# A three-layer graph network: own rows turned by transposing DMAs and joined by VectorE, in place of identity products and ScalarE copies

## What is computed

```
agg0 = segment_mean((x[src] + rel_emb[type]) @ W_msg.T + b_msg, dst)
x1   = layernorm(x + x @ W_self.T + b_self + agg0)                      # layer 0
h    = swish(segment_mean(x1[src], dst) @ W1_l.T + b1 + x1 @ W1_r.T)    # layer 1
out  = layernorm(x1 + segment_mean(h[src], dst) @ W2_l.T + b2 + h @ W2_r.T)   # layer 2
```

## Time and profile before

| | |
|---|---|
| time, median of 3 runs | 354.44 us (354.37 to 354.53) |
| time of the profiled execution | 354.82 us |
| its span in the profile | 353.0 us (1.8 us lie around it) |
| TensorE busy | 327.9 us, 93% |
| VectorE busy | 232.5 us, 66% |
| ScalarE busy | 172.2 us, 49% |
| granted TensorE clock, mean | 0.994 |

### The profile page before, as it was taken

The page is one execution under the profiler, slowest core; times in us unless marked ns, Lnnn a source line. Parts: engine busy times, 40 slices in busy tenths (PEclk is TensorE's granted clock), DMA queues, the critical chain, the costliest instruction groups (busy, mean ns, idle before and its releaser), DMA issues.

```text
span 353.0 us, 9059 instructions
## 1 busy us (share of the span) xinstructions
PE 327.9 (93%) x3319; PEld 244.3 (69%) x3319; DVE 232.5 (66%) x597; ACT 172.2 (49%) x380; POOL 4.9 (1%) x18
## 2 busy tenths in 40 slices
PE   0699999999999999999999999999999999999990
PEld 0698788998998998998994645554564655554560
DVE  6999999989999999999447893213307225225304
ACT  3586557778878778778712422312322411211220
POOL 5000000000000000000000000000000000000000
PEclk9999999999999999999999999999999999999997
DMA  4712000000000000000110000000000001001011
GB/s 138 241 32 62 2 2 9 2 4 9 3 2 8 3 2 9 3 4 2 39 42 8 2 0 0 2 0 2 0 2 1 2 30 31 2 30 31 2 32 37
DMA packets 6958, 7.30 MB, mean 21 GB/s; under 512 B 653, under 2 KB 5888, under 8 KB 6912
## 3 DMA queue, kind: packets, MB, share of 16 engines
q1 hardware_dynamic: 6624, 6.25, 6.0%
q10 hardware_dynamic: 288, 0.43, 0.3%
HBM read 4.75 MB, written 1.60 MB: 18 GB/s over the span
## 4 chain that ended last, share of the span: by engine, by line
PE 82%; DVE 5%; ACT 2%; issue 1%; ACTq 0%; DVEq 0%
PE ps L1021 37%; PE ps L1002 17%; PE ps L947 15%; PE ps L1095 5%; PE ps L1105 3%; PE ps L1040 2%; ACT counts L891 1%; DVE hot L1258 1%; PE ps L954 1%; PE ps L964 1%; DVE table L1268 1%; DVE hot L1251 0%; DVE table L1258 0%; ACT new_first L869 0%; DVE table L1330 0%
## 5 line engine op out<-in xcount | busy, mean ns | idle before, releaser
L1021 PE MATMUL ps<-counts,table 128*128 128x512 f16 (+1 forms) x736 | 135.2, 340 | 0.0
L891 ACT CAST counts<-ps 128x494 f32 x208 | 107.7, 579 | 44.1 <-PE ps L947 43.6
L1021 PEld LDWEIGHTS ps<-counts,table 128*128 128x128 f16 x736 | 60.5, 97 | 64.8 <-issue 0.2
L947 PE MATMUL ps<-hot 128*128 128x156 f16 (+1 forms) x592 | 68.9, 241 | 13.8 <-DVE hot L1258 13.3
L1002 PE MATMUL ps<-counts,table 128*128 128x256 f16 x600 | 78.2, 271 | 0.0
L947 PEld LDWEIGHTS ps<-hot 128*128 128x128 f16 x592 | 53.4, 102 | 16.9 <-DVE hot L1258 14.6
L1258 DVE TENSOR_TENSOR hot<-iota,edges 128x1200 f16<-128x1200 f16 x74 | 57.5, 777 | 0.0
L1002 PEld LDWEIGHTS ps<-counts,table 128*128 128x128 f16 x600 | 52.9, 97 | 5.5
L954 PE MATMUL ps<-window_hot,hot 128*128 128x19 f16 x296 | 43.0, 180 | 0.0
L1251 DVE TENSOR_TENSOR hot<-iota,edge_rows 128x768 f16<-128x768 f16 x74 | 40.8, 551 | 2.8 <-PE ps L984 2.3
L847 ACT ACTIVATE scaled<-ps,rdeg 128x128 f32<-128x128 f32 (+1 forms) x75 | 21.7, 373 | 24.0 <-PE ps L1095 21.6
(11 more groups left out here) (148 smaller groups left out, 324.4 us busy)
## 6 DMA issues: line engine op xcount, KB each, us to landing
own_T<-x_turned SPq DMA_DIRECT2D x4, 256.0 KB, 2.7
table<-x_rows SPq DMA_DIRECT2D x1, 832.0 KB, 5.9
table<-x_rows SPq DMA_DIRECT2D x1, 768.0 KB, 4.2
out<-new_first SPq DMA_DIRECT2D x3, 256.0 KB
out<-hot SPq DMA_DIRECT2D x3, 256.0 KB, 2.4
sum_first<-x_turned SPq DMA_DIRECT2D x2, 256.0 KB, 4.9
counts<-counts SPq DMA_DIRECT2D x6, 53.0 KB
counts<-first_dst ACTq DMA_DIRECT2D x1, 208.0 KB, 3.8
```

The costliest lines, as they stand in the source:

```text
L891: nc.scalar.copy(A[:, HALVES[half], bass.ds(bases[group % 8], GROUP_W)], window(group, half)).then_inc(copied[half], 1)
L947: return nc.tensor.matmul(window(group, half)[:, :, at[t]], row(tiles[t], LOW_AT, P), blocks_of(tiles[t], half), start=group == half == t ...
L1021: last = nc.tensor.matmul(ps[:, sums_bank(q), 0:nodes], table[:, b, which, :], A[:, b, at:at + nodes], start=b == which == 0, stop=b + 1 = ...
```

## The change

The identities (`ident_h`, `ident_stacked`), `turn` on TensorE and `turn_out` on ScalarE go. SP turns the rows instead: `turn_rows(q)` issues, per tile of 128 nodes, one transposing DMA within SBUF for the high part and one for the low part, 8 a chunk (one for the short chunk, where one tile holds both), into `turned_high` and `turned_low`. These lie on what the counting used (`window_hot` and `iota`), so the first ones wait for `opened`, TensorE's last reading of `iota`. There is one such pair of buffers; `turn_rows(q)` waits until the chunk before has been joined (`own_ready`). VectorE joins: `join(q)` adds the two parts in float16 into `x_T(q)` in float32. The division by 256 moves to the weights that meet these rows: one VectorE operation on `weights_later[:, 1:4:2]` at q = 6.

`join(q + 1)` stands in VectorE's iteration q after `add_up(q)`, ahead of `swish` or `measure`; for the short chunk ahead of `preset(q + 1)`.

```
+            def turn_rows(q):
+                sp.wait_ge(lo_ready, q - CHUNKS + 1)
+                if q > CHUNKS:
+                    sp.wait_ge(own_ready, q - CHUNKS)
+                first = chunk_of(q) * SUB
+                for t in range(tiles_of(q)):
+                    sp.dma_start(turned_high[:, t * P:(t + 1) * P],
+                                 table_in(q)[:, first + t, 0, :], transpose=True
+                                 ).then_inc(turned, 16)
+                    if tiles_of(q) > 1:
+                        sp.dma_start(turned_low[:, t * P:(t + 1) * P],
+                                     table_in(q)[:, first + t, 1, :], transpose=True
+                                     ).then_inc(turned, 16)
...
             stack_counts(EARLY + 1)
+            sp.wait_ge(opened, OPENED)
+            for q in range(CHUNKS, 2 * CHUNKS + 2):
+                turn_rows(q)
             for q in range(2 * CHUNKS, ALL_CHUNKS):
+                if q + 2 < ALL_CHUNKS:
+                    turn_rows(q + 2)
                 sp.wait_ge(rows_ready, q + 1)
...
+            def join(q):
+                dve.wait_ge(turned, turned_by(q))
+                if tiles_of(q) > 1:
+                    dve.wait_ge(dense_done, q)
+                    high, low_bits = turned_high, turned_low
+                else:
+                    dve.wait_ge(messages_done, before(q) + 1)
+                    high = turned_high[:, 0:LAST]
+                    low_bits = turned_high[:, REL_ROW:REL_ROW + LAST]
+                nc.vector.tensor_tensor(x_T(q)[:, 0:nodes_of(q)], high, low_bits, ALU.add
+                                        ).then_inc(own_ready, 1)
...
             for q in range(EARLY - 1, ALL_CHUNKS):
                 if EARLY <= q < CHUNKS:
                     degrees(q)
+                if q == CHUNKS - 1:
+                    dve.wait_ge(late_weights_in, 80)
+                    nc.vector.tensor_scalar(weights_later[:, 1:4:2, :], weights_later[:, 1:4:2, :],
+                                            1.0 / SCALE, None, ALU.mult
+                                            ).then_inc(weights_ready, 1)
...
+                joins = CHUNKS <= q + 1 < ALL_CHUNKS
+                if joins and tiles_of(q + 1) == 1:
+                    join(q + 1)
                 if q + 1 < ALL_CHUNKS:
                     preset(q + 1)
                 add_up(q)
+                if joins and tiles_of(q + 1) > 1:
+                    join(q + 1)
```

Removed in return:

```
-            def turn_out(q):
-                act.wait_ge(turned, q + 1 - CHUNKS)
-                nc.scalar.copy(x_T(q)[:, 0:nodes], ps[:, TURN, 0:nodes]
-                               ).then_inc(own_ready, 1)
-            def turn(q):
-                for t in range(tiles_of(q)):
-                    for part in range(1 if both else 2):
-                        last = nc.tensor.matmul(
-                            ps[:, TURN, t * P:t * P + size],
-                            table_in(q)[:, chunk_of(q) * SUB + t, part, :],
-                            ident_stacked if both else ident_h[:, 0:size],
```

More of the change, by code:

```diff
@@ L181, in summed_before @@
     return q - 1 if q <= EARLY else -1 if q == EARLY + 1 else q - 2
+OPENED = 1
 def stored_in(slot):
@@ L221, in gnn_program @@
         bias_first = sb("bias_rows", [P, 2, D])
-        ident_h = sb("ident_h", [P, P], F16)
         rel_ones = sb("rel_ones", [P, 2], F16)
@@ L261, in gnn_program @@
         bias_last = later[:, 4 * D + 2 * CHUNK + TILES + GROUPS:][:, 0:D]
-        ident_stacked = later[:, 5 * D + 2 * CHUNK + TILES + GROUPS:].bitcast(F16)[:, 0:LAST]
-        assert 5 * D + 2 * CHUNK + TILES + GROUPS + P // 4 <= (SLOTS - 1) * HOT_C * GROUP // 2
+        assert 5 * D + 2 * CHUNK + TILES + GROUPS <= (SLOTS - 1) * HOT_C * GROUP // 2
+        turned_high = window_hot[:].rearrange("p n h w t -> p (n h w t)")[:, 0:CHUNK]
+        turned_low = iota[:].rearrange("p c t -> p (c t)")[:, 0:CHUNK]
         ident = new_first[:, 0:P]
@@ L284, in x_T, with turned_by @@
             return own_T[:] if tiles_of(q) > 1 else sum_T(q)[:, P:P + LAST]
+        def turned_by(q):
+            full = q - CHUNKS + 1 - sum(tiles_of(k) == 1 for k in range(CHUNKS, q + 1))
+            return 16 * (2 * SUB * full + q - CHUNKS + 1 - full)
         def new(q):
@@ L317, in sums_bank @@
             return 4 if q <= EARLY or slot_of(q) else 0
-        TURN = 3
         def messages_bank(q):
@@ L843, in scale @@
                 else:
-                    act.wait_ge(weights_ready, 3)
+                    act.wait_ge(weights_ready, 2)
                 for t in range(tiles_of(q)):
@@ L913, in _ @@
                     lead(q)
-                    if q >= CHUNKS:
-                        turn_out(q)
                 if q > EARLY:
@@ L1027, in aggregate @@
                         last.then_inc(agg_done, 1)
-            def turn(q):
[L1030 to L1036, removed]
-                for t in range(tiles_of(q)):
-                    size = min(P, nodes_of(q))
-                    for part in range(1 if both else 2):
-                        last = nc.tensor.matmul(
-                            ps[:, TURN, t * P:t * P + size],
-                            table_in(q)[:, chunk_of(q) * SUB + t, part, :],
-                            ident_stacked if both else ident_h[:, 0:size],
-                            start=part == 0, stop=both or part == 1, skip_group_check=True)
-                last.then_inc(turned, 1)
             def wait_turned(q):
@@ L1089, in dense @@
                     if q == CHUNKS:
-                        pe.wait_ge(late_weights_in, 80)
+                        pe.wait_ge(weights_ready, 3)
                     if q >= POSTED:
@@ L1152, in _ @@
                     aggregate(q, range(cut, BLOCKS))
-                    turn(q)
                 else:
                     aggregate(q, range(BLOCKS))
-                    turn(q)
                     dense(q - 1, all_tiles(q - 1))
@@ L1281, in constant @@
                                             ALU.add).then_inc(weights_ready, 1)
[L1282 to L1286, removed]
+            CONSTANTS = (4, 14)
             def degrees(k):
@@ L1312, in preset @@
                 else:
-                    dve.wait_ge(opened, 1)
+                    dve.wait_ge(opened, OPENED)
                 if layer < 2:
@@ L1530, in _ @@
             wait_copied(dve, GROUPS)
-            nc.vector.tensor_tensor(ident_stacked, ident_h[:, 0:LAST],
-                                    ident_h[:, REL_ROW:REL_ROW + LAST], ALU.add
-                                    ).then_inc(weights_ready, 1)
             nc.vector.memset(table1[32:REL_ROW, BLOCKS - 1], 0.0)
```

3 lines of the change are left out of this document (removed).

## The result

The changed kernel takes 356.33 us (355.82 to 356.99, 5 runs) against 354.53 (5 runs) for the kernel before: a ratio of 1.0047 with an interval of 1.0029 to 1.0065. It is slower by half a per cent, where 350.6 was forecast and a range of 349.9 to 372.

A forecast was written before the change was run, and what follows sets the result against it. TensorE was taken to bound the kernel: 4.46 us of later turns removed, less 0.61 us net delay at dense(8), gave 354.44 - 3.85 = 350.6 us, with cheap DMAs assumed; range 349.9 to 372.

The forecast's parts named there:

- What bounds the kernel: TensorE, busy in nearly every slice and 82% of the last chain, sets the pace at 12.80 us a chunk.
- the work removed: On TensorE, each full chunk's eight turn products give 0.44 us, 5.3 us over 12 chunks; short chunks 0.03 us twice.
- The work added on VectorE: Join 0.69 us and scaling 0.40 delay TensorE 1.09 us at layer 1's start; dense(8) starts 0.61 later, net.
- The spacing c: Spacing of eight transposing DMAs on SP's queue: bounds 0.47 and 2.0 us, taken as below 0.83, near plain DMAs.
- The price at a given c: At join(7), each 0.1 us of c beyond 0.83 costs 0.7 us; beyond 1.37, the cycle costs 8.4 us.
- rival C: Nothing gained, c from 1.28 to just past 1.37: first stall or cycle eats the gain, 353.7 to 355.1; chance 0.09.
- This happens once: The first batch's lateness at join(7) stalls TensorE only once, since everything behind shifts with it.
- The ring's own sum: Join, eight DMAs, join: cycle 7c + 2.77 us from 186.5 to join(19), against TensorE's 12.36; slack used up near c 1.32.
- A: Cheap transposes, c up to 0.83: 350.6 us, or 350.2 to 351.5 with variations; chance 0.45.
- D: Transposes become the bound, c over 1.37, ring longer than TensorE's chunk: 366 us at c 1.5, 408 at 2.0; chance 0.33.
- What the profile after was to show: Layer 1 lead spacing 12.36 us, join 0.69, TensorE idle about 1 us before aggregate(7)'s last block, eight issues from 186.5.

The follow-up runs named there:

- run 2: Changed kernel without transposing DMAs, joins or weight scaling, TensorE multiplying old buffer contents: 349.61 us, ratio 0.9861 to the kernel before.
- run 1: Changed kernel without its 98 transposing DMAs and the join's wait for them, the join adding old contents: 350.87 us, ratio 0.9895 to the kernel before.
- run 13: Changed kernel with one transposing DMA for a whole chunk, 1024 columns to eight blocks: 350.54 us, ratio 0.9889 to the kernel before.
- run 12: Changed kernel with one transposing DMA for a tile's high and low part, 50 DMAs in all: 350.17 us, ratio 0.9876 to the kernel before.
- run 5: Changed kernel with the first eight DMAs issued early and join(7) and join(14) behind low(q): 351.92 us, ratio 0.9925 to the kernel before.
- run 8: Changed kernel with only join(14) moved behind low(13): 356.59 us, ratio 1.0056 to the kernel before.
- run 11: Changed kernel with each full-chunk transposing DMA turning only 64 of its tile's 128 rows: 356.51 us, one run.
- run 6: Changed kernel with first eight DMAs early, join(7) and join(14) behind low(q), and two pairs of buffers: 351.73 us, ratio 0.9911 to the kernel before.

## Why the prediction was wrong

- **What bounds the kernel, and the work removed.** Right. TensorE alone set the pace; the chunks now follow at 12.36 us, and the removal alone gives 1.4% (run 2).
- **The work added on VectorE.** Right in place, too dear in size. The join takes 0.69 us as forecast (0.691 measured) and 0.20 in place of 0.40 of the scaling shows, but `low(6)` is delayed by 0.69 us in all, not 1.09, and TensorE by 0.45 at `dense(7)` and 0.66 at `dense(8)` (runs 1 and 2, each counted from its `dense(5)`). The slack there was not nil: the prediction's own 196.01 against 196.23 leaves 0.2 us. Counted so to `dense(19)` the kernel without DMAs gains 4.4 us where 3.85 was forecast. That its median, 350.87, lies so close to the 350.6 of the sum is in part luck.
- **The spacing c: the step that failed first.** "I take c near the plain spacing, below 0.83". It is 1.27, from a fixed cost of each issue on SP. The argument "32 KB over sixteen engines that are idle" looked at the wrong resource: the engines were indeed idle, and the bytes cost next to nothing (run 13 moves eight times as much in the same 1.24 us), but the issuing queue was busy for 1.23 us. The prediction itself called c a choice and not a reading. The figure of 1309 ns that the prediction quoted from the Trainium skill ("VectorE: DVE Perf Modes", "The three transpose paths") was the better guide, near the 1.27 of the trace; but that is the spacing of issues, while a block has landed 2.4 us after its issue, and eight blocks in one DMA are issued in 1.24. The other page's statement, transposes as fast as regular DMAs ("Advanced Engine Details and Errata", "X-Bar Transpose (TRN2)"), says nothing of issues, and for them the trace has 1.27 against 0.47.
- **The price at a given c: two terms missing.** With c = 1.27 and a landing of 2.4 us the prediction's own formula gives 350.6 + 7 x 0.44 + 0.4 = 354.1, and its rival C reached to 355.1; 356.3 was measured. Missing is first the low clock behind a stall of 4 us: 1.6 us by `dense(7)`, about 1.1 after the give-back. The prediction let the stall cost its own length. Missing is second the deadline in the middle. It asked the ring to be in time for `dense(19)`; but `join(14)` stands ahead of `low(13)`, which TensorE awaits at layer 2's start, 0.9 us. With both the sum is 356.1. "This happens once" was true of the first batch and overlooked the second place of the same form.
- **The ring's own sum.** The prediction adds two short chunks of 2.35 us ahead of `join(19)`, but only q = 13 lies there, so its slack used up at c = 1.32 should read 1.35. With c = 1.27 and a landing of 2.4 the corrected sum has `join(19)` end at about 333.9 us, in time; it started at 339.05. The sum lacks the pause at `join(8)`, which came 3.0 us behind the ring because the edge checks stand ahead of it, and five issues that took 3.8 us more than the others. A cycle without such an issue is mostly 11.96 us (212.60 to 224.56), with one 12.6 to 13.0, against TensorE's 12.36: the ring had next to nothing to catch up with.
- **The rivals.** The result is C's mechanism, a late first join that eats the gain, plus these two terms. A's time is that of the kernel without DMAs and of run 12. D would have needed c over 1.37 by the prediction's arithmetic; at 1.27 its ring was already felt, by 0.9 us in the kernel after and by 1.4 us in run 5, where the first batch is early.
- **What the profile after was to show.** The chunk spacing, the join's row, the batch at 186.5 and 0.69 us were there; TensorE's idle of about 1 us was 4.1, and the spacing of the eight issues, named as the number that decides, decided.

Left open: why the low clock lasted 3.8 us in one profile and about 6 us in two others (runs 8 and 11), which alone moves `dense(8)` by 1.1 us, and why the later `join(14)` alone gave nothing in any of its runs.

## What to carry to other kernels

A transposing DMA within SBUF cost its issuing queue a fixed 1.2 to 1.3 us here, so turn many blocks with one DMA; eight blocks cost as much to issue as one. When work moves to another engine, look for what is queued behind its waits in order, above all where a layer's last result and the next layer's first preparation share an in-order engine. And when a fix of one stall gains nothing, take away the second limit with it before calling the first harmless. Last, where medians differ by less than their scatter, compare the starts of the same operations in the traces: that showed 1.4 us of the ring that the times of runs 5 and 6 hid.

## What the runs showed of the hardware

- The issue of a transposing DMA occupies SP for about 1.23 us, with 64 or 128 rows, 128, 256 or 1024 columns; the plain loads of the later weights take 0.43. Issue to landing is 2.4 us for one block and 3.1 for eight.
- Six of the 98 issues took 0.5 to 1.0 us longer (1.75 at 207.23 above). The runs don't tell why.
- Transposing DMAs beside TensorE's and VectorE's work cost neither anything that shows but waits: the ratio is 0.9876 with 50 of them and 0.9895 with none, the same within the intervals, and `dense(8)` to `dense(19)` takes 125.50 us in both.
- A stretch of 4 us with hardly a product was followed by 3.8 us at a granted clock of 0.55, in two other profiles by 6 us at 0.50 (from 200.4 to 206.4); 18 unused products in it kept the clock at 1.00.
